# Row one-hots as seventeen short comparisons, and two jobs moved between engines, in the first norm of a graph network

## The chip, the cores and the metric

The kernel runs on one core of a Trainium2 chip, as one launch. The metric is the device time of that launch in microseconds (us), the median of several runs. A core has TensorE (PE, with its weight loads shown apart as PEld), VectorE (DVE), ScalarE (ACT), GpSimd (POOL) and SyncE (SP), which here only starts DMAs.

## The reference

A graph of 50000 nodes with 64 features each, and 100000 edges in order of their target: 25000 edges, the same reversed, and a loop at each node.

```python
h = relu(layernorm(x))                                     # the first norm
e = softplus(softplus(concat(h[src], h[dst]) @ W0 + b0) @ W1 + b1) @ W2 + b2
x = x + segment_sum(e, src, N)
h = relu(layernorm(x))                                     # the second norm
z = h + segment_sum(h[src], dst, N)
z = relu(z @ gW1 + gb1) @ gW2 + gb2
x = x + h + relu(batchnorm(z) * gamma + beta)
```

The change lies in what is done beside and in the first norm. All arithmetic is in float32; small integers are also kept in float16.

## The kernel before, in words

The kernel runs in stages with a barrier between them: a survey of the edges, `prepare` (the first norm), `edges0` (the edge network and the second norm), `edges1` (the sums over neighbours), and `finish`. The nodes are cut into 49 blocks of 1024 (`BLOCKS`); a block lies in SBUF as 128 partitions by 8 groups (`SUBS`) of 64 numbers, so 128x512.

`prepare` does two things for each block. The first is the norm: the sum of each group (`sum_columns`, DVE, L577), the mean (`scale_mean`, ACT), the subtraction of the mean (`centre` on POOL for the first 6 groups, `ON_POOL`, L552, and `centre_rest` on DVE for the other 2, L582), squares (`square`, ACT), variance (`variance`, DVE, L588), the logarithm and exponential that make the inverse root (ACT), and `normalise` (8 activations on ACT, L670). The result is stored to DRAM (`store`), and PE also turns it (`turn_cols`, L630) into a PSUM bank, from which `keep_cols` copies it into the table `h0_cols` (ACT, L685).

The second is the packing of edges. The survey left five small float16 numbers for each edge in DRAM; 128 x 17 of them (`RAW` is 17) are loaded for each block (`load_raw`). DVE compares the tile number of each with the block's 9 tiles (`tile_hot`, L565, 128x153), then its place in the tile with the numbers 0 to 127 (`row_hot`, L569, 128x2176). Both are one `tensor_tensor` with broadcast operands. POOL multiplies `tile_hot` with three fields (`spread`, L544, 128x459). PE multiplies `row_hot` with `spread` in 17 matmuls (`pack`, L621), and ACT moves the result (`move`). After the last block DVE unpacks the packed table in some ten instructions (L596 to L611); PE turns one of them (L636), and it goes to DRAM for the next stage.

Each engine has its own program. `rounds(engine, stages, total)` writes it out: in round u the engine does each (lag, body) of the list, in order, for block u - lag. Engines wait for each other by counting semaphores (`wait_ge`), and buffers are reused after 4 blocks (`RING`), or 2. The lists of DVE and POOL are

```python
rounds(dve, [(0, sum_columns), (3, variance), (1, centre_rest), (0, row_hots)], BLOCKS)
rounds(pool, [(1, centre), (0, spread_fields)], BLOCKS)
```

So on POOL the centring of a block comes straight behind its spread. The loads of x and of the edge fields are started by SP when the buffers are free.

Of the kernel before, what the change touches and what calls it, by code (L numbers as in the profile page):

```python
# [8 lines left out]
ALU = mybir.AluOpType  # L9
ACT = mybir.ActivationFunctionType  # L10
# [6 lines left out]
RING = 4  # L17
# [45 lines left out]
def gnn_program(nc, x, src, dst, w0, b0, w1, b1, w2, b2, g_w1, g_b1, g_w2, g_b2, gamma, beta, out):  # L63
# [3 lines left out]
    P = 128  # L67
# [32 lines left out]
    with ExitStack() as ctx:  # L100
# [363 lines left out]
        def prepare(h0_cols):  # L464

            K = 3
            with ExitStack() as ph:
                def t(n, shape, k=RING, dt=F32):
# [21 lines left out]
                     "const_made", "row_hot_ready", "tile_hot_ready", "spread_ready", "pack_done", "packed_copied",  # L490
                     "sum_done", "mean_done", "centred_done", "squared_done", "var_done", "log_done", "rstd_done",
                     "normed_done", "unpacked"))
                cols_turned, cols_kept, rest_centred = s("cols_turned"), s("cols_kept"), s("rest_centred")
                ON_POOL = 6
                from_sub_ready, local_turned, local_moved, local_stored = (
                    s(n) for n in ("from_sub_ready", "local_turned", "local_moved", "local_stored"))
                chunks = [(i, min(P, TILES_ALL - i * P)) for i in range(-(-TILES_ALL // P))]
# [2 lines left out]
                with nc.Block("prepare") as block:  # L500
                    @block.sync
                    def _(sp):
                        def load_raw(b, q, turn):
                            wait_from(sp, spread_ready, b - RING + 1, passed_sp)
                            wait_from(sp, row_hot_ready, b - RING + 1, passed_sp)
                            start = sp.value_load(block_start[0:1, bass.ds(b, 1)], min_val=0, max_val=E)
                            sp.dma_start(raw[q][:, :], edge_fields[bass.ds(start, RAW * P), :]
                                         .rearrange("(p t) k -> p (t k)", p=P)).then_inc(raw_loaded[q], 16)

                        def load_x(b, q, turn):  # L510
                            wait_from(sp, centred_done, b - RING + 1, passed_sp)
                            wait_from(sp, rest_centred, b - RING + 1, passed_sp)
                            if is_last(b):
                                full, left = TAIL // P, TAIL % P
                                sp.dma_start(groups(xin[q][:, :], D)[:, 0:full, :], x[b * NB:b * NB + full * P, :]
                                             .rearrange("(s p) f -> p s f", p=P)).then_inc(x_loaded[q], 16)
                                sp.dma_start(xin[q][0:left, full * D:(full + 1) * D], x[b * NB + full * P:N, :])\
                                  .then_inc(x_loaded[q], 16)
                            else:
                                sp.dma_start(groups(xin[q][:, :], D), x[bass.ds(b * NB, NB), :]  # L520
                                             .rearrange("(s p) f -> p s f", p=P)).then_inc(x_loaded[q], 16)
                        rounds(sp, [(0, load_x), (0, load_raw)], BLOCKS)
                        sp.wait_ge(local_moved, 1)
                        for i, n in chunks:
                            sp.dma_start(local_t[i * P:i * P + n, :], local_rows[0:n, i * P:(i + 1) * P])\
                              .then_inc(local_stored, 16)
                        sp.wait_ge(local_stored, 16 * len(chunks))

                    @block.gpsimd
                    def _(pool):  # L530
# [18 lines left out]
                        def centre(b, q, turn):  # L549
                            hold(pool, mean_done, b + 1, passed_pool)  # L550
                            wait_from(pool, normed_done, b - RING + 1, passed_pool)
                            G.tensor_tensor(groups(centred[q][:, :], D)[:, 0:ON_POOL], groups(xin[q][:, :], D)[:, 0:ON_POOL],  # L552
                                            mean[q][:, 0:ON_POOL].unsqueeze(2).to_broadcast([128, ON_POOL, D]),
                                            ALU.subtract).then_inc(centred_done, 1)
                        rounds(pool, [(1, centre), (0, spread_fields)], BLOCKS)

# [1 line left out]
                    def _(dve):  # L558
                        V = nc.vector

                        def row_hots(b, q, turn):
                            f = groups(raw[q][:, :], FIELDS)
                            dve.wait_ge(raw_loaded[q], 16 * (turn + 1))
                            wait_from(dve, spread_ready, b - 1)
                            V.tensor_tensor(groups(tile_hot[q % 2][:, :], CT), f[:, :, 0:1].to_broadcast([128, RAW, CT]),  # L565
                                            iota_tile[:, bass.ds(b * CT, CT)].unsqueeze(1).to_broadcast([128, RAW, CT]),
                                            ALU.is_equal).then_inc(tile_hot_ready, 1)
                            wait_from(dve, pack_done, b - 1)
                            V.tensor_tensor(groups(row_hot[q % 2][:, :], P),  # L569
                                            f[:, :, 1:2].to_broadcast([128, RAW, P]),  # L570
                                            iota_h[:, :].unsqueeze(1).to_broadcast([128, RAW, P]),
                                            ALU.is_equal).then_inc(row_hot_ready, 1)

                        def sum_columns(b, q, turn):
                            dve.wait_ge(x_loaded[q], 16 * (turn + 1) + (16 if is_last(b) else 0))
                            wait_from(dve, centred_done, b - RING + 1)
                            V.tensor_reduce(mean[q][:, :], groups(xin[q][:, :], D), AX.X, ALU.add).then_inc(sum_done, 1)  # L577

                        def centre_rest(b, q, turn):
                            dve.wait_ge(mean_done, b + 1)  # L580
                            wait_from(dve, normed_done, b - RING + 1)
                            V.tensor_tensor(groups(centred[q][:, :], D)[:, ON_POOL:SUBS], groups(xin[q][:, :], D)[:, ON_POOL:SUBS],  # L582
                                            mean[q][:, ON_POOL:SUBS].unsqueeze(2).to_broadcast([128, SUBS - ON_POOL, D]),
                                            ALU.subtract).then_inc(rest_centred, 1)

                        def variance(b, q, turn):
                            dve.wait_ge(squared_done, b + 1)
                            V.tensor_reduce(var[q][:, :], groups(squared[q][:, :], D), AX.X, ALU.add)\  # L588
                             .then_inc(var_done, 1)

                        dve.wait_ge(const_made, 3)
                        rounds(dve, [(0, sum_columns), (3, variance), (1, centre_rest), (0, row_hots)], BLOCKS)

                        dve.wait_ge(packed_copied, BLOCKS)
                        f = groups(packed[:, :], K)
                        V.scalar_tensor_tensor(src_f[:, :], f[:, :, 0], 2048.0, f[:, :, 1], ALU.mult, ALU.add)  # L596
# [44 lines left out]
                    def _(act):  # L641
# [5 lines left out]

                        def square(b, q, turn):
                            act.wait_ge(centred_done, b + 1)
                            act.wait_ge(rest_centred, b + 1)  # L650
                            wait_from(act, var_done, b - RING + 1)
                            A(squared[q][:, :], centred[q][:, :], ACT.Square).then_inc(squared_done, 1)

# [26 lines left out]
                            act.dma_start(h0_t[bass.ds(b * NB, NB), :].rearrange("(s p) f -> p s f", p=P),  # L680
                                          groups(normed[q][:, :], D)).then_inc(stored[q], 16)

                        def keep_cols(b, q, turn):
                            act.wait_ge(cols_turned, b + 1)
                            A(h0_cols[:, bass.ds(b * TW, TW)], banks[4 + q % 2][:, :], ACT.Copy).then_inc(cols_kept, 1)  # L685
                        act.preload_act_table_set(EXP_LN_SET)
                        rounds(act, [(0, scale_mean), (3, log_variance), (1, square), (1, move), (3, invert), (3, normalise), (4, store),
                                     (5, keep_cols)],
                               BLOCKS)
                        act.wait_ge(cols_kept, BLOCKS)  # L690
                        for q in range(RING):
                            act.wait_ge(stored[q], 16 * ((BLOCKS - q + RING - 1) // RING))

# [1414 lines left out]
```

## Time and profile before

| | |
|---|---|
| median of 3 runs | 1985.07 us (1983.5 to 1986.97) |
| profiled execution | 1981.82 us, span 1979.3 us |
| busy, share of the span: PE | 1428.0 us, 72% |
| PE weight loads | 1067.5 us, 54% |
| VectorE | 1063.9 us, 54% |
| ScalarE | 975.3 us, 49% |
| GpSimd | 1071.2 us, 54% |
| DMA | 200.77 MB, 101 GB/s |
| `prepare` | about 78 to 310 us of the span |

The shares are means over stages in which different engines are full. In the slices of the page in which `prepare` runs, VectorE is at 9 tenths or more while PE is at 3; afterwards PE is at 9 and VectorE at 5. The end of a record can lie behind the start of the next one of the same engine, since instructions overlap at their ends; the time that an instruction costs its engine's queue is from its start to the next start.

### The profile page before, as it was taken

How to read it: one execution, taken by the hardware profiler on the slowest of the kernel's cores; microseconds unless marked ns; L12 is line 12 of the kernel's file. 1: busy time of each engine (PE TensorE's matmuls, PEld its weight loads, DVE VectorE, ACT ScalarE, POOL GpSimd, SP SyncE). 2: the span in 40 equal slices, each digit the busy share in tenths (PEclk: the TensorE clock that was granted, in tenths of full speed). 3: DMA queues.
4: the chain of work that ended last, by engine and by line, in shares of the span. 5: the costliest groups of instructions: out<-in, count | busy, mean ns of one | idle time of the engine just before them, and what ended most of it. 6: DMA issues, size and time to landing. Idle time of an engine off the chain costs nothing. (4 is left out here: it accounts for less than half of the span.)

```text
span 1979.3 us, 37799 instructions
## 1 busy us (share of the span) xinstructions
PE 1428.0 (72%) x10165; PEld 1067.5 (54%) x10165; DVE 1063.9 (54%) x3259; ACT 975.3 (49%) x2310; POOL 1071.2 (54%) x1151
## 2 busy tenths in 40 slices
PE   0033337999999999999999994666556556566566
PEld 0022225777777777777777784443434334334334
DVE  4899993555555555555555555443443433433344
ACT  0188885776777777677777763111111111111144
POOL 0388884454444445445444542776666666666600
PEclk9999999999999999999999997777777777777765
DMA  1255544444554554455455453222222222222259
GB/s 34 61 125 130 122 109 115 125 119 119 130 129 110 128 135 115 122 129 127 111 129 136 111 138 73 58 57 55 47 53 51 50 54 46 54 54 46 33 180 340
DMA packets 435913, 200.77 MB, mean 101 GB/s; under 512 B 382585, under 2 KB 408710, under 8 KB 435866
## 3 DMA queue, kind: packets, MB, share of 16 engines
q1 hardware_dynamic: 343384, 142.00, 27.7%
q0 software_dynamic: 28224, 32.57, 9.1%
q10 hardware_dynamic: 64258, 25.65, 4.5%
q8 instruction: 19, 0.31, 0.1%
q14 instruction: 28, 0.23, 0.0%
HBM read 131.49 MB, written 55.79 MB: 95 GB/s over the span
## 5 line engine op out<-in xcount | busy, mean ns | idle before, releaser
L821 POOL DMA_INDIRECT fast_gathered<-h_table,fast_gather_i x441 | 423.2, 960 | 471.8 <-PE bank L963 295.0
L1180 POOL DMA_INDIRECT fast_gathered<-h_neighbours_table,fast_index_i x441 | 425.8, 966 | 197.4 <-POOL fast_index_i L1176 104.9
L1080 ACT ACTIVATE fast_h<-bank,b_s 128x384 f32<-128x384 f32 (+1 forms) x490 | 299.7, 622 | 177.7 <-PE bank L990 140.4
L1241 PE MATMUL node_sums<-twice,fast_self_rows 128*64 128x128 f32 x784 | 139.0, 423 | 279.3 <-DMA fast_gathered<-h_neighbours_table,fast_index_i 275.2
L1241 PEld LDWEIGHTS node_sums<-twice,fast_self_rows 128*64 128x64 f32 x784 | 120.5, 222 | 317.5 <-issue 307.0
L1272 ACT ACTIVATE fast_z_in<-node_sums 128x512 f32<-128x512 f32 x49 | 29.3, 597 | 517.7 <-PE node_sums L1247 517.7
L1087 ACT ACTIVATE fast_h<-fast_h 128x384 f32<-128x384 f32 (+1 forms) x490 | 263.8, 558 | 0.0
L1226 DVE BATCH_NORM_STATS2 z_stats<-z_t (+1 forms) x48 | 33.3, 694 | 386.2 <-ACT z_t L1283 386.2
L999 PE MATMUL bank<-fast_h,w_s 128*128 128x384 f32 (+1 forms) x490 | 235.3, 562 | 2.8 <-ACT fast_h L1087 1.9
L1247 PE MATMUL node_sums<-fast_hot,fast_gathered 128*64 128x256 f32 (+1 forms) x980 | 217.4, 444 | 0.0
L1034 PE MATMUL node_sums<-fast_message,fast_hot 128*128 128x80 f32 x1568 | 200.9, 276 | 0.0
L1034 PEld LDWEIGHTS node_sums<-fast_message,fast_hot 128*128 128x128 f32 x1568 | 186.8, 192 | 0.0
L853 DVE TENSOR_TENSOR fast_message<-bank,b_s 128x192 f32<-128x192 f32 x147 | 52.6, 358 | 240.1 <-PE bank L1019 240.1
L1247 PEld LDWEIGHTS node_sums<-fast_hot,fast_gathered 128*64 128x64 f32 x980 | 143.5, 189 | 62.1 <-issue 39.4
L544 POOL TENSOR_TENSOR prep_spread<-prep_tile_hot,prep_raw 128x459 f16<-128x459 f16 x49 | 146.4, 2987 | 27.2 <-DVE prep_tile_hot L565 27.2
L968 PE MATMUL bank<-fast_dst_hot,fast_own_rows 128*64 128x128 f32 x1568 | 161.1, 278 | 0.0
L963 PE MATMUL bank<-ident,fast_gathered 128*64 128x128 f32 x882 | 152.5, 282 | 0.0
L1019 PEld LDWEIGHTS bank<-w_s,fast_h 128*128 128x128 f32 x882 | 121.5, 191 | 49.0 <-issue 16.7
L621 PE MATMUL bank<-prep_spread,prep_row_hot 128*128 128x27 f16 x833 | 30.6, 187 | 146.7 <-POOL prep_spread L544 105.7
L1192 DVE TENSOR_SCALAR fast_hot<-iota_row,far_local 128x256 f32<-128x256 f32 (+1 forms) x441 | 125.3, 362 | 17.3 <-PE node_sums L1247 12.6
L968 PEld LDWEIGHTS bank<-fast_dst_hot,fast_own_rows 128*64 128x64 f32 x1568 | 125.4, 137 | 11.3 <-issue 1.5
L843 DVE TENSOR_SCALAR fast_hot<-iota_row,far_local 128x256 f32<-128x256 f32 (+1 forms) x441 | 122.3, 334 | 0.0
(234 smaller groups left out, 2578.9 us busy)
## 6 DMA issues: line engine op xcount, KB each, us to landing
fast_local<-local_rows SPq DMA_DIRECT2D x49, 576.0 KB, 5.5
h_neighbours_table<-fast_h_rows SPq DMA_DIRECT2D x49, 320.0 KB
fast_self_rows<-h_neighbours_table SPq DMA_DIRECT2D x49, 320.0 KB, 3.3
h_table<-prep_normed ACTq DMA_DIRECT2D x49, 256.0 KB, 2.7
fast_own_rows<-h_table SPq DMA_DIRECT2D x49, 256.0 KB
fast_own_cols<-h_cols SPq DMA_DIRECT2D x49, 256.0 KB
x_plus_h<-fast_total SPq DMA_DIRECT2D x49, 256.0 KB, 6.4
finish_resid<-x_plus_h SPq DMA_DIRECT2D x49, 256.0 KB, 4.0
```

Source lines behind the costliest of these rows:

```text
L544: G.tensor_tensor(spread[q % 2][:, :].rearrange("p (t c k) -> p t c k", c=CT, k=K), groups(tile_hot[q % 2][:, :], CT).unsqueeze(3).to_broa ...
L821: pool.indirect_dma_start(gathered[slot][:, j * D:(j + 1) * D], None, h0_t, bass.IndirectOffsetOnAxis(ap=gather_i[q][:, n:n + 1], axis=0))\
L963: last = M(to, gathered[q * GK + k][:, j * D:(j + 1) * D], ident[:, :], start=True, stop=True)
L968: last = M(to, own_rows[q][:, sub * D:(sub + 1) * D], dst_hot[q][:, at:at + P], start=(sub == lo), stop=(sub == hi - 1))
L999: M(ps_2[:, 0:w], w1_s[:, :], h1[at][:, 0:w], start=True, stop=True).then_inc(pre2_done, 1)
L1034: last = M(node_sums[q][:, to:to + MW], hot[q * GK + k][:, at:at + P], message[q][:, c * MW:(c + 1) * MW], start=False, stop=(k == GK - 1 ...
L1080: A(to[at][:, 0:w], psum[:, 0:w], ACT.Exp, bias=b_s[:, :]).then_inc(done, 1)
L1087: A(to[at][:, 0:w], to[at][:, 0:w], ACT.Ln, bias=1.0).then_inc(done, 1)
L1180: pool.indirect_dma_start(gathered[q][:, c * MW:(c + 1) * MW], None, h1_t, bass.IndirectOffsetOnAxis(ap=index_i[q][:, c:c + 1], axis=0))\
L1192: last = V.tensor_scalar(hot[q % 2][:, c * HW:c * HW + (hi - lo) * P], iota_row[:, lo * P:hi * P], far_local[:, bass.ds(b * CT + c, 1)], N ...
L1241: nc.tensor.matmul(banks[6 + q % 2][h * D:(h + 1) * D, k * P:(k + 1) * P], self_rows[q][:, at:at + D], twice[:, :], start=(k == 0), stop=F ...
L1247: last = nc.tensor.matmul(banks[6 + q % 2][h * D:(h + 1) * D, (a - h * HALF) * P:(z - h * HALF) * P], gathered[q][:, c * MW:c * MW + D], h ...
```

## The change

The rows' one-hots are made by 17 `tensor_scalar` instructions of 128x128, each of which compares the numbers 0 to 127 with one number per partition. POOL centres all 8 groups, and `centre_rest` is gone with its semaphore. `keep_cols` is moved from ACT to DVE, where it is first in each round; DVE waits for all copies before it unpacks.

```diff
-                cols_turned, cols_kept, rest_centred = s("cols_turned"), s("cols_kept"), s("rest_centred")
-                ON_POOL = 6
+                cols_turned, cols_kept = s("cols_turned"), s("cols_kept")
...
-                            wait_from(sp, rest_centred, b - RING + 1, passed_sp)
...
-                            G.tensor_tensor(groups(centred[q][:, :], D)[:, 0:ON_POOL], groups(xin[q][:, :], D)[:, 0:ON_POOL],
-                                            mean[q][:, 0:ON_POOL].unsqueeze(2).to_broadcast([128, ON_POOL, D]),
+                            G.tensor_tensor(groups(centred[q][:, :], D), groups(xin[q][:, :], D),
+                                            mean[q][:, :].unsqueeze(2).to_broadcast([128, SUBS, D]),
                                             ALU.subtract).then_inc(centred_done, 1)
...
-                            V.tensor_tensor(groups(row_hot[q % 2][:, :], P),
-                                            f[:, :, 1:2].to_broadcast([128, RAW, P]),
-                                            iota_h[:, :].unsqueeze(1).to_broadcast([128, RAW, P]),
-                                            ALU.is_equal).then_inc(row_hot_ready, 1)
+                            for n in range(RAW):
+                                last = V.tensor_scalar(row_hot[q % 2][:, n * P:(n + 1) * P], iota_h[:, :],
+                                                       f[:, n, 1:2], None, ALU.is_equal)
+                            last.then_inc(row_hot_ready, 1)
...
-                        def centre_rest(b, q, turn):
-                            dve.wait_ge(mean_done, b + 1)
-                            wait_from(dve, normed_done, b - RING + 1)
-                            V.tensor_tensor(groups(centred[q][:, :], D)[:, ON_POOL:SUBS], groups(xin[q][:, :], D)[:, ON_POOL:SUBS],
-                                            mean[q][:, ON_POOL:SUBS].unsqueeze(2).to_broadcast([128, SUBS - ON_POOL, D]),
-                                            ALU.subtract).then_inc(rest_centred, 1)
...
+                        def keep_cols(b, q, turn):
+                            dve.wait_ge(cols_turned, b + 1)
+                            V.tensor_copy(h0_cols[:, bass.ds(b * TW, TW)], banks[4 + q % 2][:, :]).then_inc(cols_kept, 1)
...
-                        rounds(dve, [(0, sum_columns), (3, variance), (1, centre_rest), (0, row_hots)], BLOCKS)
+                        rounds(dve, [(5, keep_cols), (0, sum_columns), (3, variance), (0, row_hots)], BLOCKS)
+                        dve.wait_ge(cols_kept, BLOCKS)
...
-                            act.wait_ge(rest_centred, b + 1)
...
-                        def keep_cols(b, q, turn):
-                            act.wait_ge(cols_turned, b + 1)
-                            A(h0_cols[:, bass.ds(b * TW, TW)], banks[4 + q % 2][:, :], ACT.Copy).then_inc(cols_kept, 1)
...
-                        rounds(act, [(0, scale_mean), (3, log_variance), (1, square), (1, move), (3, invert), (3, normalise), (4, store),
-                                     (5, keep_cols)],
+                        rounds(act, [(0, scale_mean), (3, log_variance), (1, square), (1, move), (3, invert), (3, normalise), (4, store)],
                                BLOCKS)
-                        act.wait_ge(cols_kept, BLOCKS)
```

## Rows read from the trace of the kernel before

**Rows 1.** The windows: stretch and its length, each engine's busy us, clock, DMA.

```profile
82.00:290.00 208.00, 71.10 (x992) 53.71 (x992) 208.00 (x241) 169.30 (x640) 181.50 (x97) 1.00 0.52 120
```

**Rows 2.** The grouped lines, 0 to 380 us.

```profile
L544 POOL TENSOR_TENSOR prep_spread<-prep_tile_hot,prep_raw 128x459 f16<-128x459 f16 x49 | 146.4, 2987 | 27.2 <-DVE prep_tile_hot L565 27.2
...
L552 POOL TENSOR_TENSOR prep_centred<-prep_xin,prep_mean 128x384 f32<-128x384 f32 x49 | 40.6, 829 | 0.0
...
L685 ACT ACTIVATE h_cols<-node_sums 128x512 f32 (+1 forms) x49 | 28.2, 575 | 0.7 <-PE node_sums L630 0.7
```

**Rows 3.** The timeline of one block: start us, duration us, engine, line.

```profile
200.94 0.67 DVE L577 TENSOR_REDUCE prep_mean<-prep_xin 128x8 f32<-128x512 f32 x1
...
201.54 0.67 DVE L588 TENSOR_REDUCE prep_var<-prep_squared 128x8 f32<-128x512 f32 x1
201.81 0.82 POOL L552 TENSOR_TENSOR prep_centred<-prep_xin,prep_mean 128x384 f32<-128x384 f32 x1
...
202.13 0.65 DVE L582 TENSOR_TENSOR prep_centred<-prep_xin,prep_mean 128x128 f32<-128x128 f32 x1
...
202.70 0.31 DVE L565 TENSOR_TENSOR prep_tile_hot<-prep_raw,prep_iota_tile 128x153 f16<-128x153 f16 x1
...
202.93 2.41 DVE L569 TENSOR_TENSOR prep_row_hot<-prep_raw,iota_h 128x2176 f16<-128x2176 f16 x1
...
203.19 2.98 POOL L544 TENSOR_TENSOR prep_spread<-prep_tile_hot,prep_raw 128x459 f16<-128x459 f16 x1 [0.56 <-DVE prep_tile_hot L565]
...
205.26 0.67 DVE L577 TENSOR_REDUCE prep_mean<-prep_xin 128x8 f32<-128x512 f32 x1
...
206.13 0.83 POOL L552 TENSOR_TENSOR prep_centred<-prep_xin,prep_mean 128x384 f32<-128x384 f32 x1
```

**Rows 4.** The timeline of the second block, DVE and POOL.

```profile
85.38 0.87 POOL L552 TENSOR_TENSOR prep_centred<-prep_xin,prep_mean 128x384 f32<-128x384 f32 x1
85.48 0.94 DVE L565 TENSOR_TENSOR prep_tile_hot<-prep_raw,prep_iota_tile 128x153 f16<-128x153 f16 x1
...
86.34 2.41 DVE L569 TENSOR_TENSOR prep_row_hot<-prep_raw,iota_h 128x2176 f16<-128x2176 f16 x1
86.51 3.08 POOL L544 TENSOR_TENSOR prep_spread<-prep_tile_hot,prep_raw 128x459 f16<-128x459 f16 x1 [0.26 <-DVE prep_tile_hot L565]
```

**Rows 5.** The timeline of DVE in edges0, from 600 us.

```profile
599.96 0.80 DVE L843 TENSOR_SCALAR fast_hot<-iota_row,far_local 128x256 f32<-128x256 f32 x3
600.68 0.17 DVE L899 TENSOR_SCALAR fast_mean<-fast_mean 128x8 f32<-128x8 f32 x1
600.75 0.30 DVE L873 TENSOR_TENSOR fast_message<-slot_hot,src_mark 128x144 f32<-128x144 f32 x1
```

**Rows 6.** The grouped lines of DVE, 599.9 to 600.7 us.

```profile
L843 DVE TENSOR_SCALAR fast_hot<-iota_row,far_local 128x128 f32<-128x128 f32 x1 | 0.3, 281 | 0.0
```

**Rows 7.** The timeline in edges1: narrow windows on DVE, and POOL.

```profile
1223.31 0.35 DVE L1192 TENSOR_SCALAR fast_hot<-iota_row,far_local 128x256 f32<-128x256 f32 x1
...
1223.57 0.82 DVE L1192 TENSOR_SCALAR fast_hot<-iota_row,far_local 128x256 f32<-128x256 f32 x2
...
1224.32 0.33 DVE L1192 TENSOR_SCALAR fast_hot<-iota_row,far_local 128x256 f32<-128x256 f32 x1
...
1223.32 0.97 POOL L1180 DMA_INDIRECT fast_gathered<-h_neighbours_table,fast_index_i  x1 [0.52 <-POOL fast_index_i L1176]
```

**Rows 8.** The timeline of the end of prepare.

```profile
294.78 0.74 DVE L596 SCALAR_TENSOR_TENSOR prep_src_f<-prep_packed 128x441 f32<-128x441 f32 x1
...
299.09 0.39 DVE L608 TENSOR_SCALAR dst_mark<-dst_mark 128x441 f32<-128x441 f32 x1
...
304.05 1.06 PE L636 MATMUL node_sums<-ident,prep_from_sub 128*128 128x128 f32 x4
...
305.14 0.56 DVE L610 COPY prep_local_rows<-node_sums 128x384 f32<-128x384 f32 x1 [5.67 <-PE node_sums L636]
305.62 0.27 DVE L611 COPY prep_local_rows<-node_sums 57x128 f32<-57x128 f32 x1
```

## The prediction

> **What bounds the kernel now.** I read four views: the windows (which engine is full, stage by stage), the grouped lines of the first norm, the timeline of one of its blocks, and the same timeline where two engines meet. The chain of waits reaches back only through the last stage, so it says nothing on this one. The change is confined to the stage between 82 and 317 us, in which 49 blocks are prepared. There VectorE is busy all of the time, ACT and GpSimd about 0.81 and 0.87 of it, and PE a third of it [rows 1]. So a block costs what VectorE's queue costs. The timeline gives that queue as start-to-start steps: sum 0.60 us, variance 0.59, rest of the centring 0.57, tile one-hots (tile_hot) 0.23, row one-hots (row_hot) 2.33, together 4.32 us per block [rows 3]. The next stage starts only when this one is over, so each 0.1 us on a block is 4.8 us on the kernel.
>
> **GpSimd is less busy than it looks.** Its spread takes 2.99 us for 459 numbers, while its centring does 384 in 0.83 us [rows 2]. The reason is in the ends, not in the durations. In the steady block row_hot runs from 202.93 to 205.34 and spread ends at 206.17, 0.83 us behind it. In an early block spread starts 0.09 us sooner after row_hot, takes 3.08, and ends 0.84 us behind it all the same [rows 3, 4]. So spread sits still while VectorE's comparison with its two operands in SBUF runs, and does its work afterwards. It goes the other way too: the 128-number subtraction that starts inside GpSimd's centring takes 0.65 us and ends 0.15 us after it, and tile_hot takes 0.94 us in place of 0.31 when it starts inside the centring [rows 3, 4]. VectorE's reductions next to the same centring keep their 0.67 us. Whoever comes second waits until the other is through. Unhindered, spread is worth 459 numbers at 2.16 ns, so 0.99 us by the rate of the centring; 0.83 to 0.99 bounds it.
>
> **The change, part by part.**
>
> Removed from VectorE: the rest of the centring, 0.57 us a block, and row_hot as one instruction, 2.33 us.
>
> Added to VectorE: keep_cols, a 128x512 copy out of PSUM. The nearest rows are a 128x384 copy out of PSUM with 0.48 us to the next start [rows 8]; less 0.40 us for its 384 numbers at 1.04 ns that leaves 0.08 fixed, so 0.61 us for 512. On ACT the same copy took 0.58 us [rows 2], and that is now free there; ACT was not the bound, so it gains only in the tail.
>
> Added to VectorE: 17 comparisons of 128 float16 numbers with a one-number operand per partition. The nearest rows are the same operation in float32 in the next stage: three of them, two of 256 and one of 128, take 0.72 us from the first start to the start of what follows, at 0.26 us a step for the wide ones (0.80 less the last one's 0.28, halved), so 0.20 for 128 [rows 5, 6]. The difference is about 0.065 us for 128 numbers, which leaves 0.13 us fixed. The trace shows no such comparison in float16. Below I take the fixed part alone, 0.13 us (series 2.2 us); above the float32 step, 0.20 us (series 3.4 us). I take the middle, 0.165 us, 2.81 us for 17: already 0.48 us more than the single instruction that it replaces.
> The Trainium skill ("VectorE: DVE Perf Modes", the perf-mode tier table) says that a one-operand comparison on 16-bit numbers in SBUF handles four numbers a cycle and float32 two; the float32 step above agrees with the two, and by the page the float16 step would be about 0.16 us, an estimate.
>
> Alone, VectorE's queue would be 0.61 + 0.60 + 0.59 + 0.23 + 2.81 = 4.84 us, 0.52 more than now.
>
> Added to GpSimd: centring of 512 numbers in place of 384, 0.83 x 512 / 384 = 1.10 us. It follows on spread at once, as now (spread ends at 206.17, the centring starts at 206.13) [rows 3], because its mean was ready before the row one-hots began.
>
> **The wait that is added.** Now row_hot holds GpSimd off in one piece, and spread and centring then fall beside the reductions, which they don't disturb. Seventeen short instructions leave sixteen gaps. Spread starts 0.49 us after tile_hot starts (202.70 to 203.19), when the third comparison is due. That GpSimd gets in between instructions of a series is shown later: in a run of float32 comparisons with steps of 0.26 us, two take 0.75 us in place of 0.52 while a GpSimd instruction is under way beside them [rows 7]. Once it is in, spread keeps VectorE off for about 0.99 us and the centring behind it for 1.10, with perhaps one comparison in between. Counted from the start of tile_hot: 0.49 + 0.99 - 0.04 + 1.10 = 2.54 us until GpSimd is through, by when about 5 of the 17 are done; then 12 x 0.165 = 1.98. With keep_cols and both reductions a block costs 2.54 + 1.98 + 0.61 + 0.60 + 0.59 = 6.32 us, against 4.32: 2.00 us more. Over the 48 steps between the first block and the last that is 96 us. Queued behind the held comparisons are keep_cols, the sum and the variance of the next round, and so ACT's logarithm and the load of x; PE's pack waits for the last comparison. All of these have over a block of slack, so only VectorE's queue counts.
>
> **Head and tail.** The first five rounds have no keep_cols and the first three no variance: 5 x 0.61 + 3 x 0.59 = 4.8 us less than full rounds, of which the kernel before has some 0.3; 4.5 us to the good. At the end VectorE's unpacking ran from 294.78 to 299.48, hidden under ACT's last three blocks, and PE turned its result at 304.05 [rows 8]. It now waits for the last keep_cols, so its 4.7 us and the copy's 0.6 lie on the path, in place of PE's turn of its result, 1.1 us (304.05 to 305.14), which falls under it. The last series ends 2.0 us later, and ACT's tail of three blocks is shorter by three copies of 0.58, 1.7 us. Together 4.7 + 0.6 - 1.1 + 2.0 - 1.7 = 4.5 us lost. Head and tail cancel.
>
> The sum: the profiled execution took 1981.8 us (span 1979.3), so 2078; the median of the runs lies 3.3 us above the profiled one, so 1985 + 96 = 2081 us.
>
> **Rivals.**
> 1. *The forecast* (GpSimd gets in), chance 0.65. Its own range: comparisons at 0.13 or 0.20 us give 12 x 0.035 x 48 = 20 us either way, two comparisons more or fewer before GpSimd is through 16 us. 2050 to 2115.
> 2. *The series holds GpSimd off as row_hot did*, 0.14. For it: spread was held off for all of 2.1 us. Against: rows 7. Then spread (0.83) and centring (1.10) follow the series, beside 1.80 us of VectorE's work, and tile_hot waits the last 0.13: 0.23 + 2.81 + 1.93 = 4.97 us, +31, 2016 us. If spread gets in and the centring doesn't: 1.48 + 13 x 0.165 + 1.80 = 5.43 us, +53, 2038 (0.06).
> 3. *The float16 comparison runs at one number a cycle*, as row_hot does (2.33 us for 2176), and then, like the reductions, doesn't meet GpSimd: 0.13 + 0.13 = 0.26 us each, 4.5 for the series, 6.5 a block, +106, 2091 us; 0.07. The time alone can't tell it from the first; the duration of a comparison can.
> 4. *Faster*: the fixed part is not 0.13 but the 0.07 us that a small tensor_scalar without a one-number operand takes to the next start (600.68 to 600.75) [rows 5], and GpSimd is held off. Then 17 x 0.10 = 1.7 us, a block is 0.23 + 1.7 + 1.93 = 3.86 us, 0.46 less: 1963 us. It decides from a series under 2.3 us, 0.135 us for each comparison, and only if GpSimd stays out; with GpSimd in, even 0.10 us gives 5.5 us. All float32 rows with such an operand speak against it. 0.05, and 0.03 for a series so near 2.3 that nothing shows.
> The Trainium skill has figures for both sides: "Vector Engine (DVE) Microarchitecture Reference", measured stream behaviour, gives some 75 ns fixed per instruction, which rows 5 don't bear out where a one-number operand is read; by it a comparison would be near 0.11 us, the faster case. "SBUF — State Buffer", who interferes with whom, says that a two-port instruction and GpSimd lock each other out for whole instructions, first come first served; rows 3 and 4 agree for two-operand instructions.
>
> **How the numbers follow.** The likeliest case gives 2081. Without rival 2 more than 2 in 10 would be left out, so the range goes down to it: 2010 to 2115. A measurement of this kernel tells about 0.2% (4 us) from no change. Faster 0.05, within it 0.03, slower 0.92.
>
> **What would show it.** Comparisons of some 0.25 us with starts 0.165 apart, and one or two in each block of over 1 us, ending with GpSimd's spread or centring; spread down from 2.99 to about 1.0 us; steps between blocks of 6.3 us; VectorE still full, ACT down to about half. The prediction is wrong if spread still takes about 3 us (rival 2), if the comparisons are 0.35 us long and none is stretched (rival 3), or if starts lie 0.10 apart (rival 4).

## The result, and the profile after

The changed kernel took 2167.42 us (median of 4 runs) against 1984.28 (median of 4) for the kernel before on the same chip: a ratio of 1.0923, 95% interval 1.0904 to 1.0942, 183 us slower. The prediction had the direction, with 2081 us as the likeliest time and 2115 as the end of its range. It is wrong by 86 us, nearly half of the loss.

The stage now ends at 494 us of the span, where it ended at 311. The window of the kernel after shows that VectorE is no longer full in it. The busy times stand in the order PE, PE's weight loads, VectorE, ScalarE, GpSimd, as in [rows 1]:

```profile
82.00:290.00 208.00, 38.11 (x550) 28.97 (x551) 166.88 (x555) 78.93 (x318) 53.15 (x54) 1.00 0.30 69
```

VectorE is busy for 167 of 208 us, where it was busy for all 208 [rows 1] and was expected to stay so. What it waits for stands in the grouped lines of the stage:

```profile
L568 DVE TENSOR_SCALAR prep_row_hot<-iota_h,prep_raw 128x128 f16<-128x128 f16 x833 | 215.5, 334 | 0.0
...
L550 POOL TENSOR_TENSOR prep_centred<-prep_xin,prep_mean 128x512 f32<-128x512 f32 x49 | 50.8, 1036 | 0.0
L542 POOL TENSOR_TENSOR prep_spread<-prep_tile_hot,prep_raw 128x459 f16<-128x459 f16 x49 | 47.8, 976 | 291.2 <-DVE prep_tile_hot L563 291.2
...
L584 DVE COPY h_cols<-node_sums 128x512 f32 (+1 forms) x49 | 33.9, 691 | 88.7 <-PE node_sums L626 88.7
```

Spread is down from 2.99 us to 0.98 [rows 2], so GpSimd is no longer held off. But ahead of `keep_cols` VectorE stands idle for 88.7 us, and the releaser is PE's turn. One block of the timeline shows both, beside [rows 3]:

```profile
282.99 0.68 DVE L575 TENSOR_REDUCE prep_mean<-prep_xin 128x8 f32<-128x512 f32 x1
283.58 0.68 DVE L579 TENSOR_REDUCE prep_var<-prep_squared 128x8 f32<-128x512 f32 x1
...
284.18 0.31 DVE L563 TENSOR_TENSOR prep_tile_hot<-prep_raw,prep_iota_tile 128x153 f16<-128x153 f16 x1
...
284.40 4.40 DVE L568 TENSOR_SCALAR prep_row_hot<-iota_h,prep_raw 128x128 f16<-128x128 f16 x17
...
284.67 0.97 POOL L542 TENSOR_TENSOR prep_spread<-prep_tile_hot,prep_raw 128x459 f16<-128x459 f16 x1 [6.29 <-DVE prep_tile_hot L563]
...
285.60 1.03 POOL L550 TENSOR_TENSOR prep_centred<-prep_xin,prep_mean 128x512 f32<-128x512 f32 x1
...
288.93 0.63 PE L617 MATMUL bank<-prep_spread,prep_row_hot 128*128 128x27 f16 x17 [6.69 <-DVE prep_row_hot L568]
...
289.41 1.09 PE L626 MATMUL node_sums<-ident,prep_normed 128*128 128x128 f32 x4
...
290.75 0.69 DVE L584 COPY h_cols<-node_sums 128x512 f32 x1 [1.95 <-PE node_sums L626]
```

The last comparison ends at 288.80 and frees PE's pack, behind the pack comes the turn, and behind the turn VectorE's copy. Narrow windows on VectorE take the series of comparisons apart:

```profile
284.40 0.41 DVE L568 TENSOR_SCALAR prep_row_hot<-iota_h,prep_raw 128x128 f16<-128x128 f16 x2
...
284.73 0.96 DVE L568 TENSOR_SCALAR prep_row_hot<-iota_h,prep_raw 128x128 f16<-128x128 f16 x1
...
285.61 1.08 DVE L568 TENSOR_SCALAR prep_row_hot<-iota_h,prep_raw 128x128 f16<-128x128 f16 x1
...
288.56 0.24 DVE L568 TENSOR_SCALAR prep_row_hot<-iota_h,prep_raw 128x128 f16<-128x128 f16 x1
```

There are two comparisons of 0.25 us, one of 0.96 that ends with spread (285.69 and 285.64), one of 1.08 that ends with the centring (286.69 and 286.63), and 13 more of 0.24 us that start 0.163 apart. At the end of the stage, beside [rows 8], the unpacking now stands behind the last copy:

```profile
483.20 0.69 DVE L584 COPY h_cols<-node_sums 128x512 f32<-128x512 f32 x1 [1.94 <-PE node_sums L626]
483.93 0.75 DVE L592 SCALAR_TENSOR_TENSOR prep_src_f<-prep_packed 128x441 f32<-128x441 f32 x1
...
489.03 0.27 DVE L607 COPY prep_local_rows<-node_sums 57x128 f32<-57x128 f32 x1
```

### The profile page after: what moved, and what is told of

It reads as the page before. It is cut to its first block and busy times, and to the rows that moved or that the text cites. A ratio compares the mean times of both kernels' runs of the same rounds, so it can differ in the third digit from the quotient of the medians.

```text
span 2164.6 us, 38410 instructions
## 1 busy us (share of the span) xinstructions
PE 1428.0 (66%) x10165; PEld 1066.8 (49%) x10165; DVE 1168.7 (54%) x4043; ACT 950.1 (44%) x2261; POOL 981.8 (45%) x1151
## 5 line engine op out<-in xcount | busy, mean ns | idle before, releaser
L568 DVE TENSOR_SCALAR prep_row_hot<-iota_h,prep_raw 128x128 f16<-128x128 f16 x833 | 215.5, 334 | 0.0
L617 PEld LDWEIGHTS bank<-prep_spread,prep_row_hot 128*128 128x128 f16 x833 | 26.1, 105 | 342.8 <-issue 212.5
L542 POOL TENSOR_TENSOR prep_spread<-prep_tile_hot,prep_raw 128x459 f16<-128x459 f16 x49 | 47.8, 976 | 291.2 <-DVE prep_tile_hot L563 291.2
L1182 DVE TENSOR_SCALAR fast_hot<-iota_row,far_local 128x256 f32<-128x256 f32 (+1 forms) x441 | 124.8, 361 | 16.9 <-PE node_sums L1237 12.4
```

The source lines that it names most:

```text
L568: last = V.tensor_scalar(row_hot[q % 2][:, n * P:(n + 1) * P], iota_h[:, :], f[:, n, 1:2], None, ALU.is_equal)
L1182: last = V.tensor_scalar(hot[q % 2][:, c * HW:c * HW + (hi - lo) * P], iota_row[:, lo * P:hi * P], far_local[:, bass.ds(b * CT + c, 1)], N ...
```

## The experiments

The step of a block is the median start-to-start time of spread in the trace, and the stage's end is the start of the next stage's first gather. The chips that ran the experiments were some 35 us slower than the first one: the kernel before took 2018 to 2023 us there. In their traces 1704 to 1710 us lie behind the first gather, in the two of the first chip 1669 and 1670, so the difference lies in the later stages. The times are therefore given as ratios to the kernel before in the same runs, and the mechanism is read from steps and ends. A time marked (one) is of a single run, so it has no interval.

| kernel | step of a block, us | first gather, us | time, us | ratio to before (95%) |
|---|---|---|---|---|
| before | 4.32 | 310.8 | 1984.28 | |
| after | 8.26 | 494.2 | 2167.42 | 1.0923 (1.0904 to 1.0942) |
| e1, after with the copy on ACT | 5.73 | 378.3 | 2087.2 | 1.0342 (1.0325 to 1.0359) |
| e2, after with the copy a round later | 6.33 | 407.4 | 2115.48 | 1.0478 (1.0461 to 1.0496) |
| e3, before with the copy on DVE | 7.41 | 448.9 | 2156.86 (one) | |
| e12, the same a round later | 4.55 | 323.1 | 2034.46 (one) | |
| e4, before with the series | 5.72 | 378.0 | 2093.5 (one) | |
| e5, e2 with GpSimd behind the series | 5.08 | 350.3 | 2057.15 | 1.0187 (1.0169 to 1.0206) |
| e6, before with all centring on GpSimd | 4.33 | 311.4 | 2020.11 | 1.0009 (0.9994 to 1.0024) |
| e11, before with 4 groups on each | 4.24 | 305.9 | 2021.11 | 0.9990 (0.9978 to 1.0001) |
| e7, e2 with 64 comparisons ahead | 6.33 | 416.4 | 2123.01 (one) | |
| e8, before with paired row_hot | 3.61 | 274.9 | 1985.43 | 0.9836 (0.9817 to 0.9855) |
| e9, e2 with paired row_hot | 3.36 | 269.1 | 1981.37 | 0.9795 (0.9779 to 0.9810) |
| e10, e9 with places from ACT | 3.28 | 267.0 | 1978.94 | 0.9781 (0.9762 to 0.9801) |

In e8, e9 and e10 the steps vary from block to block, between 3.3 and 3.6 us. Over the 38 steps in the middle their means are 3.56, 3.41 and 3.37 us.

**e1: the copy back on ScalarE.** `keep_cols` as before the change, all else as after.

```diff
-                        rounds(dve, [(5, keep_cols), (0, sum_columns), (3, variance), (0, row_hots)], BLOCKS)
-                        dve.wait_ge(cols_kept, BLOCKS)
+                        rounds(dve, [(0, sum_columns), (3, variance), (0, row_hots)], BLOCKS)
...
+                        rounds(act, [(0, scale_mean), (3, log_variance), (1, square), (1, move), (3, invert), (3, normalise), (4, store),
+                                     (5, keep_cols)],
```

> The changed kernel, with keep_cols given back to ScalarE (last in its round, as before the change); the 17 comparisons and the centring on GpSimd stay. Theory A (VectorE's copy stands first in its round and waits for PE's turn, which is queued behind the pack that waits for the last comparison; 1.9 us of each block's 8.26): the idle time and the copy's 0.61 us go from VectorE's queue, 5.7 us a block (0.60 + 0.59 + 0.23 + 4.3), about 2167 - 121 = 2046 us, a few less for the tail. Theory B (VectorE is late for another reason, the short instructions and GpSimd alone): only the copy's 0.61 us goes, 7.6 us a block, about 2136 us.

The step is 5.73 us, as theory A has it, and B is out. VectorE's idle time ahead of a copy is gone, and the series is the same 4.39 us:

```profile
206.58 0.31 DVE L563 TENSOR_TENSOR prep_tile_hot<-prep_raw,prep_iota_tile 128x153 f16<-128x153 f16 x1
206.80 4.39 DVE L568 TENSOR_SCALAR prep_row_hot<-iota_h,prep_raw 128x128 f16<-128x128 f16 x17
...
211.12 0.67 DVE L575 TENSOR_REDUCE prep_mean<-prep_xin 128x8 f32<-128x512 f32 x1
```

**e2: the copy on VectorE, one round later.** This is the sharpest test of the wait, with the same instructions on the same engines and one number changed.

```diff
-                        rounds(dve, [(5, keep_cols), (0, sum_columns), (3, variance), (0, row_hots)], BLOCKS)
+                        rounds(dve, [(6, keep_cols), (0, sum_columns), (3, variance), (0, row_hots)], BLOCKS)
```

> The changed kernel, with keep_cols on VectorE for block u - 6 in place of u - 5, so that the turn it waits for lies in the round before. Nothing else. Theory A: the 1.9 us of idle time go, the copy stays: 6.34 us a block, 2167 - 92 = 2075 us. Theory B: nothing changes but one more round at the end, 2167 to 2170 us.

The step falls from 8.26 to 6.33 us, and the stage ends 87 us sooner. The copy now starts 0.22 us before PE's pack, with nothing to wait for:

```profile
208.47 0.68 DVE L584 COPY h_cols<-node_sums 128x512 f32 x1
208.69 0.63 PE L617 MATMUL bank<-prep_spread,prep_row_hot 128*128 128x27 f16 x17 [4.83 <-DVE prep_row_hot L568]
```

**e3: the copy alone, moved in the kernel before.**

```diff
-                        rounds(dve, [(0, sum_columns), (3, variance), (1, centre_rest), (0, row_hots)], BLOCKS)
+                        rounds(dve, [(5, keep_cols), (0, sum_columns), (3, variance), (1, centre_rest), (0, row_hots)], BLOCKS)
+                        dve.wait_ge(cols_kept, BLOCKS)
```

> The kernel before, with keep_cols alone moved to VectorE, first in the round for block u - 5; row_hot stays one instruction. Theory A: VectorE idles from the end of row_hot over GpSimd's rest of spread (0.83), PE's pack (0.6) and turn (1.1) and the hand-overs, some 2.75 us, and the rest of the centring no longer meets GpSimd (0.20 in place of 0.57): 2.33 + 2.75 + 0.61 + 0.60 + 0.59 + 0.20 + 0.23 = 7.3 us a block, about 2130 us. Theory B (the wait needs the long series): 4.6 us a block, about 1998 us.

The step is 7.41 us against the 7.3 of theory A, 3.09 more than before: this one move costs more than the whole series does. The wait is longer than in the kernel after (idle for 2.77 us as the median, 1.85 there), since pack waits here for the end of spread, 0.83 us behind row_hot:

```profile
208.03 2.42 DVE L569 TENSOR_TENSOR prep_row_hot<-prep_raw,iota_h 128x2176 f16<-128x2176 f16 x1
...
208.30 2.98 POOL L544 TENSOR_TENSOR prep_spread<-prep_tile_hot,prep_raw 128x459 f16<-128x459 f16 x1 [3.65 <-DVE prep_tile_hot L565]
...
211.38 0.61 PE L627 MATMUL bank<-prep_spread,prep_row_hot 128*128 128x27 f16 x17 [5.71 <-DVE prep_row_hot L569]
211.83 1.09 PE L636 MATMUL node_sums<-ident,prep_normed 128*128 128x128 f32 x4
213.09 0.69 DVE L593 COPY h_cols<-node_sums 128x512 f32 x1 [2.64 <-PE node_sums L636]
```

**e12: the same, a round later** (6 in place of 5 in e3's line).

> The kernel before, with keep_cols alone moved to VectorE, but for block u - 6, a round later than in the run that moved it alone (7.41 us a block). Theory: the wait for the turn goes and the copy covers GpSimd's centring: row_hot 2.33, copy 0.61, sum 0.60, variance 0.59, rest of the centring 0.20 with no wait, tile_hot 0.23: 4.56 us a block, so 0.24 more than before for a copy of 0.61. Rival: the wait stays for any lag, because pack always stands ahead of the turn: 7.4 us.

The step is 4.55 us. The copy's 0.60 us costs 0.22, because GpSimd's centring now falls beside the copy and the reductions, and the rest of the centring takes 0.28 us in place of 0.65 [rows 3].

```profile
205.29 0.68 DVE L593 COPY h_cols<-node_sums 128x512 f32 x1
...
206.15 0.83 POOL L552 TENSOR_TENSOR prep_centred<-prep_xin,prep_mean 128x384 f32<-128x384 f32 x1
...
207.07 0.28 DVE L582 TENSOR_TENSOR prep_centred<-prep_xin,prep_mean 128x128 f32<-128x128 f32 x1
```

**e4: the series alone, in the kernel before.** The comparison's four lines as in the change, nothing else.

```diff
-                            V.tensor_tensor(groups(row_hot[q % 2][:, :], P),
...
+                            for n in range(RAW):
+                                last = V.tensor_scalar(row_hot[q % 2][:, n * P:(n + 1) * P], iota_h[:, :],
+                                                       f[:, n, 1:2], None, ALU.is_equal)
```

> The kernel before, with the 17 comparisons alone in place of the single row_hot. Theory A (GpSimd gets in between two comparisons and holds each for as long as it works): two stretched comparisons, 0.88 and about 0.8 us apart (GpSimd centres 384 numbers here), series 4.1 us, the rest of the centring free of GpSimd, 5.7 us a block, about 2052 us. Theory B (GpSimd is held off by the series): no stretched comparison, 2.77 us for the series, about 4.9 us a block, 2012 us.

The step is 5.72 us, against the 5.7 of theory A. From the start of each of the two stretched comparisons to the next start it is 0.88 and 0.79 us. The second is 0.21 shorter than in the kernel after (1.00), as GpSimd's centring is (0.82 and 1.04).

```profile
206.65 0.31 DVE L565 TENSOR_TENSOR prep_tile_hot<-prep_raw,prep_iota_tile 128x153 f16<-128x153 f16 x1
206.88 4.18 DVE L570 TENSOR_SCALAR prep_row_hot<-iota_h,prep_raw 128x128 f16<-128x128 f16 x17
210.97 0.68 DVE L577 TENSOR_REDUCE prep_mean<-prep_xin 128x8 f32<-128x512 f32 x1
```

**e5: GpSimd kept behind the series.** On top of e2:

```diff
-                            hold(pool, tile_hot_ready, b + 1, passed_pool)
+                            hold(pool, row_hot_ready, b + 1, passed_pool)
```

> The changed kernel with keep_cols a round later, and GpSimd's spread waiting for the last comparison in place of tile_hot, so that GpSimd never works beside the series. Theory A: no stretched comparison, series 2.77 us; spread and centring then take 2.0 us behind it plus a hand-over of 0.2, and tile_hot meets the end of the centring: about 5.2 us a block, 1.1 less than with keep_cols a round later alone, about 2020 us. Rival (the stretches come from something else than GpSimd, such as the fetching of instructions): the two long steps stay, and the time is that of keep_cols a round later or more, 2075 us and up.

The step is 5.08 us. A kernel that makes GpSimd wait longer is 1.24 us a block faster than e2: both long steps are gone, and the series takes 2.84 us to the end of the last comparison. tile_hot now meets the centring (0.63 us in place of 0.31).

```profile
205.94 0.97 POOL L542 TENSOR_TENSOR prep_spread<-prep_tile_hot,prep_raw 128x459 f16<-128x459 f16 x1 [3.12 <-DVE prep_row_hot L568]
...
206.86 1.05 POOL L550 TENSOR_TENSOR prep_centred<-prep_xin,prep_mean 128x512 f32<-128x512 f32 x1
...
207.46 0.63 DVE L563 TENSOR_TENSOR prep_tile_hot<-prep_raw,prep_iota_tile 128x153 f16<-128x153 f16 x1
...
208.01 2.84 DVE L568 TENSOR_SCALAR prep_row_hot<-iota_h,prep_raw 128x128 f16<-128x128 f16 x17
```

**e6 and e11: the centring alone.** e6 is the kernel before with all eight groups on GpSimd and no `centre_rest`; e11 has one number changed:

```diff
-                ON_POOL = 6
+                ON_POOL = 4
```

> The kernel before, with all eight groups centred on GpSimd and nothing else changed. By the lock between the two engines: tile_hot takes the place of the rest of the centring as the one that waits for GpSimd; GpSimd is through 0.83 + 1.03 us after row_hot's end, tile_hot ends some 0.09 us later: 1.91 + 2.33 = 4.24 us a block against 4.32, 4 us less, about 1980 us. If moving work off VectorE's full queue were worth its 0.57 us, 3.75 us a block, 1957 us.

> The kernel before, with four groups centred on GpSimd and four on VectorE in place of six and two. By the lock: GpSimd is through 0.83 + 0.52 us behind row_hot's end, and VectorE's rest (256 numbers, 0.33 us) starts at 1.19 and waits only 0.1: 4.15 to 4.2 us a block against 4.32, 6 to 8 us less. Rival: more centring on the full engine costs what it takes, 0.13 us a block or 6 us more.

e6 gives nothing: tile_hot now starts inside GpSimd's centring, and its step of 0.81 us in place of 0.23 takes the place of the 0.57 removed:

```profile
206.18 1.04 POOL L550 TENSOR_TENSOR prep_centred<-prep_xin,prep_mean 128x512 f32<-128x512 f32 x1
...
206.51 0.89 DVE L563 TENSOR_TENSOR prep_tile_hot<-prep_raw,prep_iota_tile 128x153 f16<-128x153 f16 x1
```

The wait was foreseen, and its size was 0.1 us off; the 4 us forecast did not come. e11's step is 0.08 us shorter, where 0.12 to 0.17 was expected. The 4 us that this makes are at the edge of what the time can show (the interval reaches 1.0001). Neither rival holds: e6's step is not 3.75 us, and e11's did not grow.

**e7: prices.** The kernel of e2, with 64 comparisons ahead of the first block, while GpSimd is idle.

```diff
+                        for n in range(16):
+                            V.tensor_scalar(bench_a[:, n * P:(n + 1) * P], iota_h[:, :], 5.0, None, ALU.is_equal)
+                        for n in range(16):
+                            V.tensor_scalar(bench_b[:, n * P:(n + 1) * P], iota_h[:, :], iota_h[:, n:n + 1], None, ALU.is_equal)
...
```

> The changed kernel with keep_cols a round later, and ahead of the first block 64 comparisons on VectorE into tiles that nothing reads, while GpSimd is idle: 16 of 128 float16 numbers with a constant, 16 with a one-number operand, 16 of 128 float32 numbers with a one-number operand, 16 of 2 float16 numbers with a one-number operand. Expected from start to start: 0.10 us with the constant if the one-number operand is what costs 0.06; 0.163 with it; 0.196 in float32; 0.13 for two numbers. Rival (the fixed part belongs to every comparison): constant and one-number operand both 0.163.

```profile
80.41 1.73 DVE L591 TENSOR_SCALAR prep_bench_a<-iota_h 128x128 f16<-128x128 f16 x16 [5.65 <-POOL prep_tile_sub L537]
82.05 2.69 DVE L593 TENSOR_SCALAR prep_bench_b<-iota_h 128x128 f16<-128x128 f16 x16
84.65 3.23 DVE L595 TENSOR_SCALAR prep_bench_c<-iota_row,node_col 128x128 f32<-128x128 f32 x16
87.78 2.18 DVE L597 TENSOR_SCALAR prep_bench_d<-iota_h 128x2 f16<-128x2 f16 x16
89.85 0.69 DVE L578 TENSOR_REDUCE prep_mean<-prep_xin 128x8 f32<-128x512 f32 x1
```

Groups a and b compare 128 float16 numbers, with a constant and with a one-number operand; c compares 128 float32 numbers and d two float16 numbers, both with a one-number operand. Sixteen steps lie between one group's start and the next, so a comparison costs 0.103, 0.163, 0.196 and 0.129 us. For 128 float16 numbers the one-number operand costs 0.06 us more than the constant. With that operand a comparison of only two numbers already costs 0.129, and 126 more numbers add 0.034.

**e8: row_hot as one comparison of two dense float16 operands**, in the kernel before. This is not the change's way but what its aim, a cheaper row_hot, suggested: the place of the tile outside, the 17 edges inside.

```diff
+                            V.tensor_copy(place[q % 2][:, :], f[:, :, 1]).then_inc(place_ready, 1)
...
-                            V.tensor_tensor(groups(row_hot[q % 2][:, :], P),
-                                            f[:, :, 1:2].to_broadcast([128, RAW, P]),
-                                            iota_h[:, :].unsqueeze(1).to_broadcast([128, RAW, P]),
+                            V.tensor_tensor(groups(row_hot[q % 2][:, :], RAW), iota_pairs_g,
+                                            place[q % 2][:, :].unsqueeze(1).to_broadcast([128, P, RAW]),
...
-                                last = nc.tensor.matmul(banks[q][:, 0:CT * K], row_hot[q % 2][:, n * P:(n + 1) * P],
+                                last = nc.tensor.matmul(banks[q][:, 0:CT * K], groups(row_hot[q % 2][:, :], RAW)[:, :, n],
```

> The kernel before, with row_hot written in another order: place in the tile outside, the 17 edges inside, so that both operands of the one comparison (17 place numbers made dense by a small copy, and a table of 0 to 127 each 17 times) are dense float16 in the innermost dimension; PE reads its weights with a step of 17 numbers. Theory: two numbers a cycle, row_hot 1.2 us in place of 2.33 to the next start, the small copy 0.1: VectorE 3.3 us a block, so that ScalarE (3.7 us) becomes the bound: 3.8 to 3.9 us a block, about 1962 us. Rival: one number a cycle as now, and PE's weight loads longer: 2.33 us stays, about 4.45 us a block, 1990 us.

The step is 3.61 us, and the stage ends 36 us sooner. That is better than the 3.8 to 3.9 us expected. row_hot takes 1.35 us in place of 2.41. PE's 17 weight loads, now with a step of 17 numbers, take 1.11 us in place of 0.54, which PE has room for (88 of 150 us busy). ScalarE is busy for 144 of 150 us (fourth busy time in the second fence), and waits for other engines for only 2.3 us of it. VectorE shows as busy all of the time, but part of that is waiting inside its records: the small copy takes 0.83 us in one block and 0.17 in the next, by whether it meets GpSimd's centring.

```profile
204.60 0.31 DVE L569 TENSOR_TENSOR prep_tile_hot<-prep_raw,prep_iota_tile 128x153 f16<-128x153 f16 x1
...
204.82 1.35 DVE L574 TENSOR_TENSOR prep_row_hot<-prep_iota_pairs,prep_place 128x2176 f16<-128x2176 f16 x1
```

```profile
90.00:240.00 150.00, 88.29 (x877) 72.64 (x878) 150.00 (x256) 143.84 (x575) 120.05 (x86) 1.00 0.69 150
```

**e9 and e10: the change's two moves on top of that.** e9 is e2 with e8's row_hot in place of the series. e10 also takes the small copy of the places from VectorE to ScalarE (the diff is against e9):

```diff
-                            V.tensor_copy(place[q % 2][:, :], f[:, :, 1]).then_inc(place_ready, 1)
...
+                        def make_place(b, q, turn):
+                            act.wait_ge(raw_loaded[q], 16 * (turn + 1))
+                            wait_from(act, row_hot_ready, b - 1)
+                            A(place[q % 2][:, :], groups(raw[q][:, :], FIELDS)[:, :, 1], ACT.Copy).then_inc(place_ready, 1)
```

> The row_hot of the paired order (one comparison of two dense float16 operands), now in the changed kernel: keep_cols on VectorE a round later, all centring on GpSimd. With the paired order alone ScalarE had been busy 144 of 150 us; without the copy it has room. VectorE: copy, sum and variance 1.79 us, while GpSimd ends 0.90 - 0.04 + 1.04 = 1.90 us behind row_hot; the small copy of the places meets its end, then tile_hot 0.23 and row_hot 1.27: about 3.5 us a block against 3.61 with the paired order alone and 4.32 before; 39 us under the kernel before. Rival: ScalarE was not what mattered, and the longer centring shows: 3.8 us a block, 25 us under.

> As the kernel with all moved and the paired order, with the small copy of the places (17 numbers a partition) on ScalarE, first in its round. Then tile_hot is what meets the end of GpSimd's centring: 1.90 + 0.09 + 1.27 = 3.3 us a block, 49 us under the kernel before. Rival: ScalarE's queue brings the places late, since its round u waits for work of the round before, and VectorE waits for them: over 3.6 us a block.

The steps are 3.36 and 3.28 us as medians, 3.41 and 3.37 as means, against 3.5 and 3.3 expected. e10 takes 0.9781 of the kernel before, 44 us less where 49 was expected, and beats both kernels. With row_hot short, the moves pay. Two things speak for it in the traces, and no run takes them apart: ScalarE was nearly full in e8, and VectorE's copy now covers GpSimd's centring. In a short round of e10 VectorE's queue has no wait:

```profile
203.16 1.35 DVE L571 TENSOR_TENSOR prep_row_hot<-prep_iota_pairs,prep_place 128x2176 f16<-128x2176 f16 x1
204.43 0.68 DVE L587 COPY h_cols<-node_sums 128x512 f32 x1
205.03 0.67 DVE L578 TENSOR_REDUCE prep_mean<-prep_xin 128x8 f32<-128x512 f32 x1
205.63 0.67 DVE L582 TENSOR_REDUCE prep_var<-prep_squared 128x8 f32<-128x512 f32 x1
206.22 0.31 DVE L566 TENSOR_TENSOR prep_tile_hot<-prep_raw,prep_iota_tile 128x153 f16<-128x153 f16 x1
206.44 1.35 DVE L571 TENSOR_TENSOR prep_row_hot<-prep_iota_pairs,prep_place 128x2176 f16<-128x2176 f16 x1
```

In about every second block the copy still starts 0.1 us late, just behind the end of PE's turn (200.99 here). That looks like the same wait again, now that a round is so short:

```profile
199.89 1.10 PE L632 MATMUL node_sums<-ident,prep_normed 128*128 128x128 f32 x4
...
201.15 0.69 DVE L587 COPY h_cols<-node_sums 128x512 f32 x1
```

## Why the prediction was wrong, step by step

**The step that failed** is the sentence on what is queued behind the held comparisons: "All of these have over a block of slack, so only VectorE's queue counts." `keep_cols` has none. In round u VectorE copies the columns of block u - 5 first. PE turns block u - 5 in its round u - 1 (its lag is 4), behind `pack` of block u - 1, and that waits for the last comparison of block u - 1, which is the instruction just ahead of the copy on VectorE. So the copy always waits for pack, turn and hand-overs: 0.63 + 1.09 us less their overlap, and what lies between. VectorE is idle for 1.85 us of a block as the median, and its queue grows by 1.93. On ScalarE, last in the round, the same wait was covered by other work. The lags are in the code ahead of the prediction; I looked at how many blocks each buffer allows and not at the order of PE's queue. e2, e3 and e12 show it: with the lag alone changed the step goes from 8.26 to 6.33, and from 7.41 to 4.55. The 87 us that e2 takes off the stage are the 86 by which the forecast was wrong.

**The queue of VectorE without that wait** was right: 6.32 us forecast, 6.33 in e2. That it fits to a hundredth is luck in part, since errors cancel: GpSimd is through 2.45 us after the start of tile_hot, not 2.54, and 13 comparisons are left then, not 12. Measured one by one, the parts are series +1.40 (e4) and centring +0.01 (e6), both on the kernel before, and copy 0.60 on the changed kernel (e2 less e1); together 2.01, and 4.32 + 2.01 = 6.33. That sum takes its parts from two kernels: on the kernel before, the copy without its wait costs only 0.22 (e12). The wait adds 1.93.

**The series** was right in each term: 0.163 us a comparison for 0.165; spread 0.97 us once free for 0.99; the centring 1.04 for 1.10; both get in, at the third and the fourth comparison. I had five comparisons done when GpSimd was through, one of them between its two instructions; four were, and none lay between. e5 shows that GpSimd is the cause: kept out, the series is 1.55 us shorter to its end. The Trainium skill ("SBUF — State Buffer", who interferes with whom) says that a `tensor_scalar` too can take the ports that VectorE shares with GpSimd, and that the engine that comes second is then blocked for the other's whole instruction. The trace agrees for GpSimd ahead: a comparison of 0.96 us beside a spread of 0.97.

**The copy** was 0.60 to 0.61 us, as forecast.

**Head and tail** cancel as I had it only where the wait is gone: in e2 the steps take 4.1 us less than 48 full ones, and from the last spread to the next stage it is 4.8 more than before. In the kernel after they don't cancel. From the first spread to the last the kernel after takes 384.7 us, 11.6 less than 48 full steps (I had 4.8), since the first four steps (5.06 to 5.73 us) have neither the copy nor its wait. From the last spread to the next stage it is 27.7 us against 21.2, 6.5 lost where I had 4.5. The unpacking does lie on the path, from 483.93 to 489.30: the first gather starts 4.93 us behind its end, as in the kernel before. In all the 48 steps cost 48 x 3.93 = 188.8 us, less 11.3 at the head (11.6 less the 0.3 of the kernel before), plus 6.5 at the tail, and the first spread starts 0.6 sooner: 183.4 us. That is what the stage's end moved, and the time grew by 183.1.

**The rivals.** That the series holds GpSimd off is out (e4, e5). That the comparison runs at one number a cycle is out: its step is 0.163 us, and two in each block are stretched. The faster case needed comparisons 0.10 us apart and GpSimd kept out. A constant operand would have given the first (0.103 us, e7), the one-number operand costs 0.06 more, and GpSimd was not kept out. The edge of that case, a series of 2.3 us, was also set too high by its own terms: with 0.23 ahead and 1.93 behind, 4.32 is reached at 2.16. By the 75 ns that the Trainium skill gives as fixed ("Vector Engine (DVE) Microarchitecture Reference", measured stream behaviour) a comparison would have been near 0.11, an estimate; the constant's 0.103 agrees with that, the one-number operand's 0.163 doesn't. Missing from the list was a rival for the moved copy: a wait on another engine's queue.

## What to carry to other kernels

When an instruction is moved to another engine, follow its input back through the whole queue of the engine that makes it, not only to the instruction that makes it: if something ahead of that waits for the engine you move to, the loop is closed and each round pays its length. Slack in buffers is no slack in queues; one more round of lag was worth 87 us here. And cutting one long instruction into many short ones opens gaps for an engine that the long one kept waiting: what that engine then takes falls inside the series, 1.55 us of a block here.

## What the runs showed of the hardware

- A float16 comparison with a one-number operand read from SBUF steps at 0.129 us for 2 numbers and 0.163 for 128; with a constant it is 0.103 for 128, and in float32 with a one-number operand 0.196 (e7).
- GpSimd gets in between two of these comparisons and holds the next one until its own instruction ends: steps of 0.88 and 1.00 us beside GpSimd instructions of 0.97 and 1.04 (kernel after), and none with GpSimd kept out (e5).
- A `tensor_tensor` comparison of 2176 float16 numbers takes 2.41 us with one operand broadcast in the innermost dimension (before) and 1.35 with both operands dense in it, though one of them still repeats in the outer dimension (e8).
- PE loads weights of 128 float16 numbers with a step of 17 numbers at about half the rate: 17 of them take 1.11 us (e8) in place of 0.54.
